# Four attention and feed-forward layers on one core: wide queries made turned by TensorE, heads paired, ternary tails joined

## What is computed

```python
# attention of layer 0: 32 heads of 8 features, rotary positions
logits = jnp.einsum('bqhd,bkhd->bhqk', q, k) * scale
w = jax.nn.softmax(logits, axis=-1)
attn = jnp.einsum('bhqk,bkhd->bqhd', w, v).reshape(b, n, 256)
return attn @ Wout + bout

# feed-forward of layer 2: ternary weights, 682 hidden features
h1 = x @ w1q.T ; h3 = x @ w3q.T
return (silu(h1) * h3) @ w2q.T

# attention of layer 3: 16 heads of 128 features
q = rmsnorm((hidden_states @ Wq).reshape(B, Sq, 16, 128), gq)
k = rmsnorm((encoder_hidden_states @ Wk).reshape(B, Skv, 16, 128), gk)
attn = softmax(einsum('bqhd,bkhd->bhqk', q, k) / sqrt(128))
out = einsum('bhqk,bkhd->bqhd', attn, v).reshape(B, Sq, 2048) @ Wo
```

## Time and profile before

| | |
|---|---|
| median of 3 runs (lowest, highest) | 2075.73 us (2074.39, 2076.0) |
| the profiled execution, its own time | 2073.72 us |
| its span in the trace | 2071.8 us |
| granted TensorE clock, mean | 0.99 of 2.4 GHz |
| PE busy | 1968.2 us, 95% |
| PEld busy | 1533.0 us, 74% |
| DVE, ACT, POOL busy | 1684.7, 1276.6, 779.6 us |

### The profile page before, as it was taken

One profiled execution on the slowest core, in us unless ns is written; L12 is line 12 of the kernel. 1 busy time (PEld: TensorE's weight loads), 2 busy tenths in 40 slices (PEclk: granted clock), 3 DMA queues, 4 the chain that ended last, 5 costly groups with the idle time before them and its releaser, 6 DMA issues.

```text
span 2071.8 us, 46041 instructions
## 1 busy us (share of the span) xinstructions
PE 1968.2 (95%) x16038; PEld 1533.0 (74%) x16038; DVE 1684.7 (81%) x4558; ACT 1276.6 (62%) x3230; POOL 779.6 (38%) x1160
## 2 busy tenths in 40 slices
PE   5999999999999999998998999999899999999998
PEld 3666799899988888887987777887465566555656
DVE  6777899999789997766555788896788988888887
ACT  2778988888855455444654666644666566646661
POOL 7332030000012232222117887022877556646640
PEclk8999999999999999999999999999999999999999
DMA  9400210000045353432211120033667454545540
GB/s 343 140 2 3 78 52 2 2 2 2 13 139 192 113 169 97 133 115 74 91 65 37 29 68 2 2 126 121 223 211 226 133 167 154 186 149 183 170 127 28
DMA packets 223518, 215.75 MB, mean 104 GB/s; under 512 B 25926, under 2 KB 197992, under 8 KB 222264
## 3 DMA queue, kind: packets, MB, share of 16 engines
q1 hardware_dynamic: 197048, 129.17, 20.6%
q0 software_dynamic: 26240, 83.65, 11.2%
HBM read 115.73 MB, written 96.99 MB: 103 GB/s over the span
## 4 chain that ended last, share of the span: by engine, by line
PE 50%; DVE 24%; POOL 8%; issue 7%; DMA 5%; ACT 3%; SPq 3%; DVEq 0%; POOLq 0%; ACTq 0%
PE pb L1135 3%; PE pb L1268 3%; PE pb L1158 3%; PE pb L1107 3%; PE pb L1091 3%; PE pb L1036 3%; PE pb L1009 3%; SPq L873 2%; PE pb L1216 2%; PE pb L1143 2%; PE pb L1150 2%; PE pb L1207 2%; PE pb L1277 2%; PE pb L1100 1%; DMA turn3k<-areaA 1%
## 5 line engine op out<-in xcount | busy, mean ns | idle before, releaser
L2462 POOL TENSOR_SCALAR sm<-sm 128x1 f32<-128x1 f32 x128 | 33.5, 262 | 457.9 <-DVE sm L1752 457.3
L1517 ACT ACTIVATE areaB<-i128h,workB 128x128 f16<-128x128 f16 x512 | 156.3, 392 | 0.9 <-DVE workB L1997 0.6
L1544 ACT ACTIVATE workA<-workA 128x128 f32<-128x128 f32 x256 | 99.5, 390 | 64.0 <-DVE workA L2044 63.8
L1680 ACT ACTIVATE workA<-pb,workA 128x128 f32<-128x128 f32 x256 | 113.8, 457 | 34.5 <-DVE workA L2343 33.0
L1325 PE MATMUL pb<-areaA,workA 128*128 128x256 f32 x512 | 121.7, 382 | 3.8 <-ACT workA L1671 3.7
L1091 PE MATMUL pb<-areaB 128*128 128x128 f32 x1024 | 124.7, 277 | 0.3 <-ACT workB L1507 0.3
L1135 PE MATMUL pb<-xT,areaA 128*128 128x128 f32 x1024 | 124.7, 276 | 0.0
L1135 PEld LDWEIGHTS pb<-xT,areaA 128*128 128x128 f32 x1024 | 119.6, 192 | 5.4 <-issue 5.3
L1469 ACT ACTIVATE areaA<-pb 128x512 f32<-128x512 f32 x192 | 104.9, 603 | 28.7 <-PE pb L1009 28.2
L1325 PEld LDWEIGHTS pb<-areaA,workA 128*128 128x128 f32 x512 | 95.0, 190 | 36.5 <-issue 13.6
L1158 PE MATMUL pb<-areaA,workA 128*128 128x256 f32 x512 | 120.4, 382 | 0.5 <-DVE x L1767 0.5
(11 more groups left out here) (421 smaller groups left out, 5790.9 us busy)
## 6 DMA issues: line engine op xcount, KB each, us to landing
turn<-workA POOLq DMA_DIRECT2D x64, 256.0 KB, 2.7
workA<-turn SPq DMA_DIRECT2D x256, 64.0 KB, 2.0
turn3q<-workA POOLq DMA_DIRECT2D x64, 256.0 KB, 2.7
workB<-turn3q SPq DMA_DIRECT2D x256, 64.0 KB, 2.2
turn3k<-areaA POOLq DMA_DIRECT2D x64, 256.0 KB, 2.8
workA<-turn3k SPq DMA_DIRECT2D x256, 64.0 KB, 2.2
turn3p<-areaA POOLq DMA_DIRECT2D x64, 256.0 KB, 2.7
rows_in<-areaB SPq DMA_DIRECT2D x7, 2048.0 KB, 16.8
```

Of the source, the lines that this page charges most:

```text
L1517: m = eng.activation(u.far[:, g], i128h[:, :], ACT.Square, bias=u.at[b % 2][:, 8 * c + g:8 * c + g + 1])
L1544: m = eng.activation(u.P[i][:, h], u.P[i][:, h], ACT.Exp, accum_out=u.den[i][:, h:h + 1], bias=u.nm[i][:, h:h + 1])
L1680: m = eng.activation(u.P[i][:, h], p[:, h * 128:(h + 1) * 128], ACT.Exp, accum_out=u.den[i][:, h:h + 1], bias=u.nb[i][:, h:h + 1], scale=u ...
```

## The change

Three edits and a new table of orders.

1. **Stage 6.** `q` now has Wq as the stationary operand, four heads by two halves, and `xT` (128 columns) as the moving one, so the queries come out with features on partitions, turned as `sc` needs them. It always fills bank 0. ScalarE reads the bank twice: squares into `u.sqq`, and a copy times gq into `u.qT`. A new step `sq` on TensorE multiplies the squares by ones, in four products that each fill 32 output partitions (bank 3, shared with `xT`); VectorE's `nq` is now a block transposition of 128x128 from that bank, and GpSimd reads column 0 of it before its two short operations. The queries' trip through DRAM (`tq`, 64 GpSimd and 256 SyncE DMAs, one VectorE transposition per chunk) and the summing `nq` are gone. `pn`'s multiplication of 128x512 moves from GpSimd to VectorE, behind the reciprocal.
2. **Stage 0.** The values of heads h and h+16 now lie 8 and 16 columns apart in the stationary operand's 32, and all eight parts of `pv` accumulate into one bank `o`. `ot`, `tb` and `norm` run once per tile instead of twice; Wout's rows are permuted on the host to fit.
3. **Stage 5.** The 42 last features of w3 and of w1 stand side by side in the sign matrix, with 22 zero columns between, so one group of 106 takes the place of two of 42. Half of ScalarE's second activation now waits for the `h3` bank too.

`rk` in stage 3 has one more wait (`m_pos` of the tile before), and all five strings of `ORDER` are new.

```diff
@@ BANKS @@
-    (0, "pv"): lambda b, c: {0: (("oa", 7),), 4: (("ob", 2),)}.get(c, ()),
-    (0, "tb"): lambda b, c: ((("ra", 7),), (("rb", 2),))[c],
+    (0, "pv"): lambda b, c: (("o", 7),) if c == 0 else (),
+    (0, "tb"): lambda b, c: (("r", 2),),
...
-    (6, "q"): lambda b, c: (("q", (0, 3)[c % 2]),),
+    (6, "q"): lambda b, c: (("q", 0),),
+    (6, "sq"): lambda b, c: (("sq", 3),),
@@ TensorE, stage 0 @@
-                        k = (c - c0) * (E // 32) + E * j // 128
+                        k = c % 4 if s == 0 else (c - c0) * 2 + j // 2
                         m = eng.matmul(p[r, k * 128:(k + 1) * 128], vt[:, h, :], P[:, j * 128:(j + 1) * 128],
-                                       start=True, stop=True)
+                                       start=(s == 4 or c == 0), stop=(s == 4 or c == 7))
@@ TensorE, stage 5 @@
-                        for m_ in range(4 if c == 0 else 2):
-                            mt = 4 * c + m_
-                            M = 42 if mt == 5 else 128
+                        tiles = [(128 * m_, at + 128 * (4 * c + m_), 128) for m_ in range(4 if c == 0 else 1)]
+                        if c == 1 and tag == "h3":
+                            tiles.append((128, 640, 106))
@@ TensorE, stage 6 @@
-                    eng.matmul(p[:, :], xT[:, 0], w.wq[:, 0, c * 512:(c + 1) * 512], start=True, stop=False)
-                    eng.matmul(p[:, :], xT[:, 1], w.wq[:, 1, c * 512:(c + 1) * 512], start=False,
-                               stop=True).then_inc(full(6, "q", b, c)[0], 1)
+                    for h in range(4):
+                        for k in range(2):
+                            m = eng.matmul(p[:, h * 128:(h + 1) * 128], w.wq[:, k, (4 * c + h) * 128:(4 * c + h + 1) * 128], xT[:, k],
+                                           start=(k == 0), stop=(k == 1))
+                    m.then_inc(full(6, "q", b, c)[0], 1)
...
+                elif step == "sq":
+                    t.wait_ge(*freed(6, "q", b, c))
+                    p = room(6, "sq", b, c)
+                    for j in range(4):
+                        m = eng.matmul(p[32 * j:32 * j + 32, 0:128], ones_sq[:, 0:32], u.sqq[i][:, :, 32 * j:32 * j + 32], start=True,
+                                       stop=True)
+                    m.then_inc(full(6, "sq", b, c)[0], 1)
@@ ScalarE, stage 6 @@
-                    eng.activation(u.sqq, bank(6, "q", b, c)[:, :], ACT.Square).then_inc(freed(6, "q", b, c)[0], 1)
+                    if two:
+                        a.wait_ge(*full(6, "sq", *two))
+                        a.wait_ge(*full(6, "sc", *two))
+                    eng.activation(u.sqq[i], p4, ACT.Square)
+                    eng.activation(u.qT[i], p4, ACT.Copy, scale=gp[:, 0:1]).then_inc(freed(6, "q", b, c)[0], 1)
@@ VectorE, stage 6 @@
-                    eng.tensor_reduce(msq, u.sqq.rearrange("p (h n) -> p h n", h=4), AX.X, ALU.add).then_inc(S["l3_msq"], 1)
+                    eng.transpose(u.sT[i], bank(6, "sq", b, c)[:, 0:128].rearrange("p (h n) -> p h n", n=32)
+                                  ).then_inc(freed(6, "sq", b, c)[0], 1)
...
-                    eng.reciprocal(u.rec[i], u.den[i]).then_inc(S["l3_rec"], 1)
+                    eng.reciprocal(u.rec[i], u.den[i]).then_inc(*v.mark())
+                    v.settle()
+                    eng.tensor_tensor(u.P[i], u.P[i], bc(u.rec[i], 2, [128, 4, 128]), ALU.mult).then_inc(S["l3_pn"], 1)
@@ GpSimd, stage 6 @@
-                if step == "tq":
-                    eng.dma_start(turn3q[n % 4], u6.Dq[n % 2].rearrange("p (j w) -> p j w", j=4)).then_inc(S[f"l3_qw{n % 2}"], 16)
...
-                elif step == "pn":
-                    g.wait_ge(S["l3_rec"], nth(b, c, 4))
-                    P, rec = u6.P[c % 2], u6.rec[c % 2]
-                    eng.tensor_tensor(P, P, bc(rec, 2, [128, 4, 128]), ALU.mult).then_inc(S["l3_pn"], 1)
```

More of the change, by code:

```diff
@@ L371, in program @@
         turn3k = [nc.dram_tensor(f"turn3k_{k}", (128, 4, 128), F32).ap() for k in range(4)]
-        turn3q = [nc.dram_tensor(f"turn3q_{k}", (128, 4, 128), F32).ap() for k in range(4)]
         turn3p = [nc.dram_tensor(f"turn3p_{k}", (128, 4, 128), F32).ap() for k in range(4)]
@@ L401, in program @@
         u0.P = [carve(512) for _ in range(RP)]
-        u0.OTs = [carve(1024) for _ in range(2)]
+        u0.OTs = [carve(512) for _ in range(2)]
         u0.OT = [carve(256).rearrange("p (k n) -> p k n", k=2) for _ in range(2)]
         u0.rec = carve(32)
+        u0.O = [carve(256) for _ in range(2)]
         carve = carver(work[0])
@@ L609, in program @@
         carve = carver(work[0])
-        u6.sqq = carve(512)
+        u6.sqq = [carve(512).rearrange("p (h n) -> p h n", n=128) for _ in range(2)]
+        u6.sT = [carve(128).rearrange("p (h n) -> p h n", n=32) for _ in range(2)]
         u6.sqk = carve(512)
         u6.kn = carve(512)
-        u6.Dq = [carve(512) for _ in range(2)]
         u6.qT = [carve(512).rearrange("p (h n) -> p h n", n=128) for _ in range(2)]
-        u6.qr = [work[1][:, 8704 + 512 * k:9216 + 512 * k] for k in range(2)]
         u6.kT = [carve(512) for _ in range(2)]
@@ L1041, in small_heads @@
                         m.then_inc(S["l0_pvd" if s == 0 else "l2_pvd"], 1)
+                elif step == "tb" and s == 0:
+                    t.wait_ge(*freed(0, "o", b))
+                    p = room(0, "r", b)
+                    for k in range(4):
+                        m = eng.transpose(p[:, k * 128:(k + 1) * 128], u.OTs[b % 2][:, k * 128:(k + 1) * 128], ident)
+                    m.then_inc(full(0, "r", b)[0], 1)
                 elif step == "tb":
@@ L1459, in small_heads @@
                     if b >= RV:
-                        a.wait_ge(*full(0, "ob", b - RV, 4))
-                    eng.copy(u.vt[b % RV][:, :, 0:8], bank(0, "v", b)[:, 0:256].rearrange("p (h e) -> p h e", e=8)
+                        a.wait_ge(*full(0, "o", b - RV))
+                    eng.copy(u.vset[b % RV][:, :, :, 0:8], bank(0, "v", b)[:, 0:256].rearrange("p (a h e) -> p a h e", a=2, e=8)
                              ).then_inc(freed(0, "v", b)[0], 1)
@@ L1470, in small_heads @@
                                    scale=1.0 / math.sqrt(hd)).then_inc(freed(s, tag, b, at)[0], 1)
+                elif step == "ot" and s == 0:
+                    a.wait_ge(*full(0, "o", b))
+                    if b >= 2:
+                        a.wait_ge(*full(0, "r", b - 2))
+                    eng.copy(u.OTs[b % 2], bank(0, "o", b)[:, :]).then_inc(freed(0, "o", b)[0], 1)
                 elif step == "ot":
@@ L2257, in ternary @@
                     q = min(j, 2)
-                    r, m, sign = raw[0:rows, lo:hi], w.tmp[0:rows, 0:hi - lo], w.sign[0:rows, lo:hi]
+                    r, m, sign = raw[held[j], lo:hi], w.tmp[held[j], 0:hi - lo], w.places[j]
+                    if j < 2:
+                        r, m = (ap.rearrange("p (k n) -> p k n", k=2) for ap in (r, m))
                     v.settle()
```

254 lines of the change are left out of this document (120 added, 134 removed), and 12 rows, old and new, of tables (STEPS, TAKEN).

## The result

| | median us | runs | ratio to before, 95% interval |
|---|---|---|---|
| before | 2075.02 (2074.39 to 2078.05) | 7 | |
| changed | 2085.05 (2081.59 to 2093.51) | 7 | 1.0052 [1.0037, 1.0066] |
| changed, measured again (r1 below) | 2074.34, beside 2070.12 for before | 12 and 23 | 1.0018 [1.0006, 1.0030] |

By the ratios (their distance from 1 times the median of before) the kernel is slower, by 10.8 us in the first comparison and by 3.7 in the second. I had forecast 17 us faster. The range 2034 to 2088 holds the time, the sign is wrong. That the two comparisons differ by more than their intervals is part of what has to be explained.

The account below looks back on a forecast made before the run. TensorE was taken to bound all three stretches, VectorE close behind in the last. Terms -7.8 (stage 0), -6.0 (stage 5) and -3.5 (stage 6) made -17.3 us, forecast 2058 us; range 2034 to 2088, the forecast's own 2047 to 2069.

Parts of the forecast that it names:

- The sum: Whole kernel: stage 0, stage 5 and stage 6 together -17.3 us, giving 2058 us.
- The rest: New orders outside the three stretches: steps only exchanged with near neighbours, no cost, 5 us either way.
- Stage 0: One group of four transpositions per tile goes, 0.49 us times 16 tiles: -7.8 us, bounds 0 and 10.
- rival E: Stage 0 or 5 not bound by TensorE, or new order loses the gain there: 2066 or so, chance 0.06.
- Stage 5: Two groups of 42 become one of 106, 96 products fewer on TensorE: -6.0 us, bounds -6 and 0.
- Stage 6, the work: TensorE's added products in stage 6: q +5 us and sq +23 us, together +28 us.
- Stage 6, the waits: Wait for the queries' read back goes, 20.5 us; half of the other two waits, 11 us.
- B: VectorE bounds the last stretch, added products cost nothing, its 27 us come out whole: 2035, chance 0.15.
- C: Stage 6: sc waits for the turned keys as long as for the queries before: 2079, chance 0.20.
- D: Stage 6: q always in bank 0, TensorE stops for ScalarE's passes, 32 us: 2090, chance 0.17.
- the worst case of the sum: Stage 6: waits only change their names and all of the added work shows, +28 us.
- The signs: Profile after: stage 0 ends near 202 us; sq 23 us busy; last stretch VectorE below 84%, TensorE 97% or more.

Follow-up runs that it names:

- r1: The changed kernel without any edit, measured again against the kernel before: 1.0018, median 2074.34 us.
- e3: The changed kernel with the old order from the start to the first k of stage 6, all three edits kept, against the kernel before: 1.0037.
- s56: Stage 5's and stage 6's edits together, stage 0 as before, old order to the end of stage 5, new behind, against the kernel before: 1.0026.
- e1: The changed kernel with the old order only from the end of the experts to the end of stage 5, against the kernel before: 1.0033.
- s6: Only stage 6's edit, old order to the end of stage 5 and new order behind it, against the kernel before: 1.0023.
- the doubled sums: Stage 6's edit alone with each chunk's four products of ones and squares issued twice, against the kernel before: 1.0091.
- f1: The kernel before with idle products put on TensorE at eight places where it stands, against the kernel before: 1.0009.
- r2: The changed kernel with idle products at eight places where TensorE stands, measured again against the kernel before: 1.0011.

## Why the prediction was wrong

**The sum.** Mine was -7.8 (stage 0), -6.0 (stage 5), -3.5 (stage 6), 0 within 5 for the rest. The edits alone measure +2.9, -4.3 and +4.8: +3.4 together, and the changed kernel had +3.7 in the second comparison. That these agree is in part luck: the same three edits in the old order (e3) measured +7.7, and stages 5 and 6 together (s56) +5.4 where the two alone make +0.5. The first comparison has 7 us more than the second. Its profile is 9 us longer in stages 4 and 5 than r1's; the cause of that is open. **The rest**, "no cost", fails where it could be tested: the new order of stages 4 and 5 costs the kernel before 8.1 us [5.0 to 11.2]. In the changed kernel no such cost shows: e1 and e3, in the old order, have 1.0033 and 1.0037, which lies between the two ratios of the changed kernel. Why is open.

**Stage 0** is the largest error. The failed step is "times 16 tiles = 7.8 us on the engine that is busy 98.4%": I took the busy share for a bound, though I had written in the paragraph above that busy TensorE is not full TensorE. The second engine's share (79) says nothing of the chain through both. The stage gave 2.9 under the old order and nothing under the new, and the whole kernel with this edit alone was 2.9 slower. My lower bound of 0, "TensorE only looks full", came nearest, and I gave it 0.06 as rival E.

**Stage 5**: 6.0 against 4.3 [2.5 to 6.2]; the step holds, if a little over-sized.

**Stage 6, the work** was right: 122.1 us for 992 of `q`'s records, and 1.79 us per chunk from its start to the next product, where I had 1.80; 0.35 for `sq`, where I had 0.36. From the changed kernel's timeline:

```profile
1701.43 1.95 PE L1303 MATMUL pb<-xT,areaA 128*128 128x128 f32 x16
1703.22 1.02 PE L1332 MATMUL pb<-areaA,workA 128*128 128x512 f32 x2
```

**Stage 6, the waits** is the second failed step, "That is 20.5 us". I took it from the waits of weight loads, which pass partly under a product still under way. What TensorE itself stood before `sc` was 13.5 us, and before `wo` and `k` 3.8 each, 21.1 in all, not 42.6. All its idle time in the stretch was 32.1; I spent 31.5 of these, as if nearly every gap would close. 25 closed in s6. 28 of work less 25 of gaps is +3, measured +4.8 [2.7 to 6.8].

**The rivals.** B (VectorE bounds): no, the doubled sums cost 14 us. The page Perfetto Trace Analysis of the Trainium skill (Identifying the Most-Contended Engine) would have given TensorE room in the last stretch, its weight loads at 58% before and 70% now; that 14 of 23 added us came through decides against it there. C (the keys' trip): no, `sc` stood for nothing. D (one bank for `q`): slower is what came, but not by this; `q` stood 1.0 us in all, for a copy of `xT`. No rival of mine said that the waits would all go as wished and still be worth less than the work, though the worst case of the sum, +28, held it. **The signs** for `sq`, `sc`, `q`, VectorE's share and TensorE's 97% all came as the forecast wanted, and only the end of stage 0 (211.9 us, not 202) spoke against it: a sign must be one that a rival would not show.

## What to carry to other kernels

Before work is added to the engine that bounds a stretch in exchange for its waits, set the work against that engine's own idle time in the window, not against the waits of its loads: here 28 us of products bought back 25. A busy share of 98% on a pipelined engine does not say that taking work off it shortens the stage. Doubling the work shows only half: 15 us more cost 11, 7 us less gave 3 and, in another order, nothing. Where two profiles of one program are to be had, compare these first, and believe no stage's loss that only one shows. Do not expect ratios of single edits to add up: stages 5 and 6 together lay 0.0024 above the product of the two. And where norms are summed by products with ones, one operand type less wide was worth more (8.7 us) than either edit around it; stage 5's edit alone (0.9979) and stages 5 and 6 with bfloat16 sums (0.9984) beat both kernels.

## What the runs showed of the hardware

- Behind stops of TensorE the profiles often show a low clock: 0.50 behind 5.9 us at 971 us (before) and behind 2.5 us at 1154 us (changed, first profile), but 1.00 behind 2.6 us at 225.7 us (before). L949's two records were 1.02 us apart at the low clock, 0.43 at the full one (2.4 GHz). Keeping TensorE occupied raised the mean granted clock from 0.989 to 0.994 (f1, r2), and the time followed little or not at all (f1 +0.0009, r2 0.0007 under r1).
- Four products with 32 stationary columns, each in its own 32 partitions, take 0.35 us in float32 (eight records) and 0.18 in bfloat16 (four); eight records of 128 stationary columns take 0.90.
- VectorE's transposition of 128x128 out of PSUM took 304 ns (I had estimated 250), where 128x512 took 702.
- The same pair of kernels gave ratios of 1.0052 and 1.0018 in two comparisons, with intervals 0.0029 and 0.0024 wide that do not overlap. The intervals hold the spread between runs of one comparison, not what differs from one comparison to another.
